# Attention of a decoder block: fewer and wider transfers, row maxima split on GpSimd before they are transposed, row scores in four one-head buffers

## What is computed

```python
q = (x @ Wqa @ Wqb).reshape(b, s, 16, 16)                 # 16 heads of 16 numbers
kv = (x @ Wkva @ Wkvb).reshape(b, s, 4, 16, 2)            # 4 heads of keys and values
q, k = _rope(q), _rope(kv[..., 0]); v = kv[..., 1]
k, v = jnp.repeat(k, 4, axis=2), jnp.repeat(v, 4, axis=2) # each serves a group of 4 query heads
scores = jnp.einsum('bqhd,bkhd->bhqk', q, k) * scale
scores = jnp.where(causal, -jnp.inf, scores)
out = jnp.einsum('bhqk,bkhd->bqhd', jax.nn.softmax(scores), v).reshape(b, s, 256) @ Wout + bout
```

## Time and profile before

| | us |
|---|---|
| median of 3 runs (lowest to highest) | 1511.91 (1509.64 to 1512.24) |
| the profiled execution, its own time | 1514.28 |
| its span in the profile | 1512.5 |
| PE busy with matmuls | 1118.5 (74%) |
| DVE busy | 787.8 (52%) |
| ACT busy | 659.5 (44%) |
| POOL busy | 341.5 (23%) |

### The profile page before, as it was taken

The page is one execution under the profiler, slowest core; times in us unless marked ns, Lnnn a source line. Parts: engine busy times, 40 slices in busy tenths (PEclk is TensorE's granted clock), DMA queues, the critical chain, the costliest instruction groups (busy, mean ns, idle before and its releaser), DMA issues. The chain is left out here.

```text
span 1512.5 us, 22735 instructions
## 1 busy us (share of the span) xinstructions
PE 1118.5 (74%) x7069; PEld 811.0 (54%) x7069; DVE 787.8 (52%) x1406; ACT 659.5 (44%) x1130; POOL 341.5 (23%) x466
## 2 busy tenths in 40 slices
PE   4773367777777786456543669999999999999875
PEld 2442123333333332356442558787777878787764
DVE  4886344555555551354424346565564646573623
ACT  1333034445545555213221344656556474746342
POOL 1432344553222222100101022112030404040300
PEclk9677578999999998657855879999999999999987
DMA  2333322221111100313433020303030202010000
GB/s 76 94 106 104 120 88 82 81 85 65 59 57 58 57 18 18 110 43 127 167 137 116 1 98 1 111 0 111 0 111 0 97 14 97 14 55 15 1 15 15
DMA packets 58876, 99.28 MB, mean 66 GB/s; under 512 B 8568, under 2 KB 43136, under 8 KB 54720
## 3 DMA queue, kind: packets, MB, share of 16 engines
q1 hardware_dynamic: 55852, 91.83, 18.1%
q0 software_dynamic: 1920, 6.03, 1.3%
q10 hardware_dynamic: 1044, 0.66, 0.2%
HBM read 62.45 MB, written 35.65 MB: 65 GB/s over the span
## 5 line engine op out<-in xcount | busy, mean ns | idle before, releaser
L777 ACT ACTIVATE p_probs<-p_psS 128x512 f32<-128x512 f32 (+1 forms) x352 | 187.6, 558 | 239.0 <-ACTq L776 239.0
L692 DVE TENSOR_REDUCE p_mx<-p_psA 128x2 f32<-128x1024 f32 (+3 forms) x256 | 202.3, 822 | 171.6 <-DVEq L691 171.6
L807 PE MATMUL p_psA<-p_ks,p_qs 96*128 96x384 bf16 (+3 forms) x512 | 142.7, 331 | 79.1 <-PEq L803 79.1
L1709 DVE TENSOR_TENSOR p_hl<-p_h,p_hh 128x512 fp32r<-128x512 f32 x128 | 87.0, 689 | 155.5 <-DVEq L1708 153.5
L827 PE MATMUL p_psS<-p_qs,p_ks 99*128 99x256 bf16 (+3 forms) x512 | 125.0, 318 | 41.4 <-PEq L852 41.4
L717 POOL TENSOR_SCALAR_AFFINE_SELECT p_probs<-p_probs 128x512 f32<-128x512 f32 x128 | 81.1, 634 | 240.0 <-POOLq L716 197.2
L1594 ACT ACTIVATE p_h<-p_psG,w_columns 128x512 f32<-128x512 f32 x128 | 88.3, 690 | 99.7 <-ACTq L1593 99.3
L807 PEld LDWEIGHTS p_psA<-p_ks,p_qs 96*128 96x128 bf16 x512 | 53.9, 105 | 127.5 <-issue 114.6
L809 PE MATMUL p_psA<-p_mask_b,p_ident_b 128*128 128x128 bf16 x512 | 111.8, 237 | 0.0
L1920 PE MATMUL p_psY<-p_n,p_hh 128*128 128x256 f32 x512 | 104.6, 288 | 3.0 <-PEq L1980 2.7
L827 PEld LDWEIGHTS p_psS<-p_qs,p_ks 99*128 99x128 bf16 x512 | 43.6, 100 | 112.7 <-issue 103.2
(11 more groups left out here) (246 smaller groups left out, 2766.5 us busy)
## 6 DMA issues: line engine op xcount, KB each, us to landing
p_n<-n_parts SPq DMA_DIRECT2D x16, 1024.0 KB, 6.7
n_parts<-p_nh SPq DMA_DIRECT2D x8, 1024.0 KB, 3.9
n_parts<-p_nl SPq DMA_DIRECT2D x8, 1024.0 KB, 6.0
q_parts<-p_part SPq DMA_DIRECT2D x96, 64.0 KB
p_qs<-q_parts SPq DMA_DIRECT2D x32, 192.0 KB
o_sums<-p_o SPq DMA_DIRECT2D x128, 34.0 KB
p_x<-in_x_dram SPq DMA_DIRECT2D x8, 512.0 KB, 4.0
p_qs<-q_parts SPq DMA_DIRECT2D x32, 128.0 KB
```

The lines of the kernel that those rows point to most:

```text
L692: nc.vector.tensor_reduce(mx[:, h:h + 2, i], psA[buffer_of(g, n)][:, :, 0:P * (i + 1)], AX_X, ALU.max).then_inc(A_free, 1)
L777: nc.scalar.activation(probs[:, g % 2, at:at + n * w], psS[(g * UNITS + s) % SB][:, 0:n * w], ACT.Exp, scale=SCALE).then_inc(exp_done, 1)
L807: nc.tensor.matmul(psA[buf][:, z, 0:n], qs[0:SROWS, k, h, i * P:(i + 1) * P], ks[0:SROWS, k, g, 0:n], start=True, stop=False)
L1709: nc.vector.tensor_tensor(hl[:, s, :], h[:, s, :], hh[:, s, :].bitcast(F32), ALU.subtract).then_inc(h_parts, 1)
```

## The change

Self-attention and the stores that feed it are written differently; nothing else is touched.

1. *Transfers.* SP issues 28 a batch in attention instead of 56. The queries are loaded as before, three transfers a group. Keys and values are loaded for two groups at once (L612, L615 of the changed kernel), four transfers for each half of a batch; those of the first two batches are issued by ACT. The maxima go with one transfer of 48 rows, `3x16x128` (L637). The result goes with one store of all 128 partitions (L643) into a scratch tensor of that shape. The scratch tensors of queries, keys and values are laid out anew, and projection stores a batch with 10 transfers, not 16.
2. *Maxima.* POOL splits `mx` into three parts as it stands, four operations on 128x16 (`split`), between the third and the fourth triangle of the group. PE transposes all three parts with one bfloat16 matmul (L833) into a bank of the ring `psS`, after row unit 0 of the next group; ACT copies them (`mrows`), SP moves them. They are turned one group ahead of their use, not two. DVE has no part in it any more.
3. *Row scores.* Four one-bank buffers `psA`, each with its own `A_free` and its own reduction: 16 reductions a group of one head each, not 8 of two.
4. *SP's order* in group g: maxima of g+1, store of g-1, refill. The queries of batch 1 are loaded in the groups of batch 0, not in front of it.

```diff
-                sp.dma_start(scr["v"][b].rearrange("g p n -> p g n"),
-                             v[:, k].rearrange("p g t n -> p g (t n)")).then_inc(v_out[k], 16)
+                sp.dma_start(scr["v"][b], v[:, k].rearrange("p g t n -> p (g t n)")).then_inc(v_out[k], 16)
...
-                            for z in range(2):
-                                g = 2 * u + z
-                                sp.dma_start(scr["q"][i, g, :, b, :].rearrange("d (h t) -> h d t", h=G),
-                                             part[i][z * G * D:(z + 1) * G * D, n, :]).then_inc(parts_out[n], 16)
+                            heads = slice(u * P // D, (u + 1) * P // D)
+                            sp.dma_start(scr["q"][i, :, b, heads, :].rearrange("d h t -> h d t"),
+                                         part[i][:, n, :]).then_inc(parts_out[n], 16)
...
-        psA = [ps(f"psA{i}", [P, 2, S]) for i in range(2)]
+        psA = [ps(f"psA{i}", [P, S]) for i in range(4)]
...
-                queue.dma_start(ks[rows, k, g, :], scr["k"][0:n, g * D:(g + 1) * D, b, :]).then_inc(stack_in[k][g], 16)
+                queue.dma_start(ks[rows, k, two].rearrange("p g t -> p (g t)"),
+                                scr["k"][0:n, b, :, two].rearrange("i d g t -> i d (g t)")).then_inc(kv_in[k][z], 16)
...
-                                 scr["q"][pq, g, :, b, :].unsqueeze(0).broadcast_to([n, D, G * S])).then_inc(stack_in[k][g], 16)
+                                 scr["q"][pq, :, b, heads, :].rearrange("d h t -> d (h t)").unsqueeze(0).broadcast_to([n, D, G * S])
+                                 ).then_inc(q_in[k][g], 16)
...
-                for i in range(MROWS):
-                    row = SROWS + i
-                    sp.dma_start(qs[row:row + 1, k, g * G:(g + 1) * G, :].rearrange("o h (t q) -> o (h t) q", t=TT),
-                                 mparts[i][:, g, :]).then_inc(m_in[g], 16)
+                sp.dma_start(qs[SROWS:SROWS + MROWS, k, g * G:(g + 1) * G, :].rearrange("i h t -> i (h t)"), mrows[:, g, :]
+                             ).then_inc(m_in[g], 16)
...
-                for r in range(G):
-                    sp.dma_start(scr["o"][b, g * G + r], o[32 * r:32 * r + D + 1, g % 2, :]).then_inc(o_out[g % 2], 16)
+                sp.dma_start(scr["o"][b, g], o[:, g % 2, :]).then_inc(o_out[g % 2], 16)
...
+            def split(g):
+                rows = mx[:, g * G:(g + 1) * G, :].rearrange("p h t -> p (h t)")
+                hi, mid, low = (msplit[:, g, i, :] for i in range(MROWS))
...
+            def maxima(bank, g):
+                pe.wait_ge(split_ready, 1)
+                pe.sem_inc(split_ready, -1)
+                nc.tensor.matmul(bank[0:MROWS * NG, 0:P], msplit[:, g].rearrange("p i x -> p (i x)"), ident_b[:, :],
+                                 start=True, stop=True).then_inc(S_ready, 1)
```

More of the change, by code:

```diff
@@ L597, in attend_phase, with place, load_keys @@
         ROWS_AT = [0, 1, 2, 3, 4, 6, 7, 8]
-        MAX_AT = 10
+        RING = len(SUNITS) + 1
+        TURN = 1
+        def place(s, turn=True):
+            return s + 1 if turn and s >= TURN else s
         block = ctx.enter_context(nc.Block())
-        def buffer_of(g, unit):
-            return (g * (len(AUNITS) + 1) + unit) % 2
-        def load_keys(queue, b, k, g):
+        def load_keys(queue, b, k, z):
+            two = slice(z * KVH // 2, (z + 1) * KVH // 2)
             row = 0
@@ L655, in batch @@
                         if has_next:
[L656 to L660 removed]
+                            refill(b + 1, 1 - k, KVH - 1)
+                    if first and g + 1 < KVH:
+                        load_queries(1, 1, g + 1)
             for g in range(KVH):
                 load_queries(0, 0, g)
[L664 to L667 removed]
+            maxima(0, 0)
+            load_queries(1, 1, 0)
             batch(0, 0, True, True, True)
@@ L782, in batch @@
                             out((g - 1) % KVH)
-            batch(True)
-            with act.Fori(1, B):
-                batch(False)
+            maxima(psS[0], 0)
+            batch(True, True)
+            with act.Fori(1, B - 1):
+                batch(False, True)
+            batch(False, False)
             out(KVH - 1)
@@ L860, in batch @@
-                    pe.sem_inc(m_in[g], -(16 * MROWS))
-                    for s in range(UNITS):
-                        n = start + s
-                        if n >= SB:
-                            exps(n - SB + 1)
-                        elif not first:
-                            exps(max(x for x in range(KVH * UNITS) if x % SB == n % SB) + 1 - KVH * UNITS)
-                        score_cols(k, g, s)
+                    pe.wait_ge(m_in[g], 16)
+                    pe.sem_inc(m_in[g], -16)
@@ L869, in batch @@
+                    for s in range(len(SUNITS)):
+                        if turn and s == TURN:
+                            maxima(ring(TURN, start), (g + 1) % KVH)
+                        score_cols(ring(place(s, turn), start), k, g, s)
                         if rows and s in ROWS_AT:
                             score_rows(*ahead, ROWS_AT.index(s))
-                        if rows and s == MAX_AT:
-                            maxima(ahead[1])
                         if s == PV2_AT and (g >= 1 or not first):
@@ L883, in batch @@
                             values(k, g, 1)
-                assert used[0] == WAITED
-            for g in range(AHEAD):
-                for unit in range(len(AUNITS)):
-                    score_rows(0, g, unit)
-                maxima(g)
+                return KVH * RING - (0 if has_next else 1) - used[0]
+            for unit in range(len(AUNITS)):
+                score_rows(0, 0, unit)
+            maxima(psS[0], 0)
+            pe.wait_ge(exp_done, 1)
+            pe.sem_inc(exp_done, -1)
@@ L890, in _ @@
+            for unit in range(len(AUNITS)):
+                score_rows(0, 1, unit)
             pe.wait_ge(minus_set, 1)
```

229 lines of the change are left out of this document (117 added, 112 removed).

## The result

The changed kernel takes **1454.1 us** in the median (1451.6 to 1457.7), the one before 1512.1 (1509.6 to 1515.7) beside it: ratio 0.9616, interval 0.9588 to 0.9645. The forecast was 1446, with a range from 1426 to 1478, and a chance of 0.96 for a faster kernel. The profiled execution took 1451.6 us with a span of 1449.8, the one before 1514.3 with 1512.5.

The account below looks back on a forecast made before the run. The first DMA engine, 306 KB or 12.0 us a group, was taken as the bound. Terms for groups, first batch, start and end summed to -65.7 us: 1514.3 to 1448.6 profiled, so 1446 us median, range 1426 to 1478.

Parts of the forecast that it names:

- The bound before: In steady groups the first DMA engine passes 306 KB at 26 GB/s, 12.0 us, setting the period of 12.2.
- The group after: Critical cycle between PE's matmuls of the maxima: 10.6 us a group, from 9.6 to 11.9.
- (b): PE's waits for row-score buffers ahead of units 4 and 6: 0.5 of 1.33 us left, bounds 0 and 1.33.
- (d): POOL's new split on 128x16, with hand-offs: 1.4 us a group, bounds 0.9 and 2.2.
- The new wait at L833: PE idle about 1.3 us a group ahead of the maxima's matmul, until POOL's split ends.
- the start: Start of attention: 5.5 us from fewer stores, 5 back for batch 1's keys, row scores 4; -4, bounds 0 and -9.
- The quicker row scores some 4: Before the first maxima: quicker first row scores bring the start some 4 us forward.
- Later phases: Phases after attention: no changed transfer on their path, so 0 us.
- A: POOL's split is shorter or hidden: groups of 9.6 to 10.0 us, kernel 1422 or 1434 us; chance 0.17.
- B: First DMA engine still sets the pace: maxima land late, refilled groups 11.7 us, kernel 1471 us; chance 0.14.
- C: Slower than before: maxima landing in 11 us make groups of 14.4 us, kernel 1551 us; chance 0.03.
- D: Something unseen holds groups at 12.2 us; only start, first batch and end change, 1490 to 1510 us; chance 0.04.

Follow-up runs that it names:

- run 1: The kernel before with the wide store alone, one transfer of 128 rows a group instead of four of 17: 1467.1 us, ratio 0.9694.
- run 2: The changed kernel with the four stores of 17 rows put back and the scratch tensor in its old shape: 1511.9 us, ratio 0.9993.
- run 7: The changed kernel with query transfers cut to 16 rows each without the broadcast, six a group instead of three: 1439.8 us, ratio 0.9515.
- run 3: The changed kernel with the first copy of POOL's split made three times, a longer split: 1483.5 us, ratio 0.9804.
- run 4: The changed kernel with POOL's split moved ahead of the third triangle: 1432.5 us, ratio 0.9462.
- run 6: The changed kernel with PE's matmul of the maxima one step later: 1440.4 us, ratio 0.9516.
- run 8: The changed kernel with the second batch's keys and values issued by SP behind the first maxima, not by ACT at the start: 1445.5 us, ratio 0.9562.
- run 5: The changed kernel with row scores in two buffers of two heads again, each freed by one reduction: 1481.2 us, ratio 0.9781.
- run 12: The kernel before with the wide store and four row-score buffers of one head, keeping the old split and two groups of lead: 1434.2 us, ratio 0.9456.
- run 11: The kernel of run 9 with the split's four operations on DVE behind its last reduction, not on POOL: 1429.4 us, ratio 0.9446.
- run 9: The changed kernel with the split ahead of the third triangle and query and key transfers cut to 16 rows: 1403.2 us, ratio 0.9287.

## Why the prediction was right, and where it was off

- **The bound before**: right. Runs 1 and 2 move 120 KB a group off or on one engine, and groups go between 12.2 and 10.8, between 10.4 and 12.3. The sum for run 2, 309 KB at 26 GB/s or 12.1 us, comes within 2%. The trace doesn't name the engine of a packet: that one engine is full follows from packet counts, sizes and these runs. The number of transfers, changed with it, is excluded by run 7.
- **The group after**: forecast 10.6, measured 10.43. (b) the buffers' waits: 0.5 left forecast, 0.31 measured. (d) the split: 1.4 forecast, 1.36 measured. The new wait at L833: 1.3 forecast, 1.05 measured. Run 3 shows that it is serial, run 4 that most of it goes once the split is moved, run 6 that it goes when the turn is later and mostly comes back at the values. That half of what the buffers give is paid back was low: 0.73 of 1.09. The upper bound of the group's sum, 11.9, doesn't follow from its terms: with no wait gone and the split at 2.2 they add up to 12.2. DVE's busy time was forecast to rise to 7.7 us a group and stayed at 6.8 (81.18/12; 6.9 before), so this sign of being right did not appear; nothing hung on it, since DVE doesn't set the group.
- **The sums**, measured against forecast: steady twelve -21.3 (-19.2), eight with weights -19.8 (-18), six further -6.7 (-5.5), last two +1.8 (+2), first batch -14.6 (-16), end -6.1 (-5, from the last exponential to the next phase).
- **The step that failed is the start**: -4 forecast, +1.4 measured, outside its bounds of 0 and -9. With the later phases it makes 8.2 us, of which the better groups gave back 5; the profiled execution missed by 3.0 (1451.6 against 1448.6), so that the close total is in part luck: two errors offset each other. Two of its three terms came out: SP free 5.6 earlier (5.5), and the keys of the second batch 5.0, by run 8 (5). The first came out by luck, since twelve transfers fewer at 0.58 us would be 7.0 and not 5.5. "The quicker row scores some 4" is the term that failed. PE did finish sooner: it is through with what stands ahead of the first step at 186.2, 33.3 us after attention begins, where the first step came after 35.9 us before. But it then waited 7.94 us for the landing, so that nothing of this counts: the first step comes 41.3 us after the beginning, and 40.2 to 41.2 in runs 2 to 6, which have the same loads. The forecast added up gains and losses of two paths, PE's and the transfers', of which only the longer one sets the start. What stood ahead of the landing were keys (run 8) and queries of four groups, as run 7 shows by spreading them, -9.5. Not in the forecast at all was a longer gap before attention begins, 4.0 us and not 2.4. Its cause stays open, but it goes with the changed projection: the kernels with the old stores there have 2.4 to 2.6 (before, runs 1 and 12), all others 3.8 to 4.4.
- **Later phases**: 0 forecast, +2.8 measured. Kernels whose code is the same from there on scatter as much: from the last exponential to the end of the span 909.6 us in run 8, 919.2 in run 7, 914.2 in the changed kernel, with a mean granted clock of 0.73, 0.71 and 0.71 in the first 369 us of it. I ascribe nothing to the change there. The beginning of attention scatters as well, from 149.5 to 153.8 us in the eleven kernels with the changed projection, so that a start is better counted from there.
- **Rivals.** A's time of 1434 came true, but by moving the split (run 4), not in the change itself. B was wrong for the steady stretch (run 7: 12 groups in 125.6 with 81 KB) and right for the start and the first batch, where its mechanism cost 14 us; I had priced it at the wrong place. C and D fell: groups are 10.4 with maxima landed in time.

The Trainium skill's rule that a leading broadcast of c copies confines a transfer to at most c engines ("DMA: Bandwidth & Descriptors", "Use all 16 engines") speaks against a form that the change keeps. Run 7 agrees, with 14.3 us; what decides is that these transfers stand ahead of something waited for, since in the steady groups the same cut gives nothing.

## What to carry to other kernels

Add up the bytes of each transfer by the engines that it is really shared by, and look at the fullest one; a mean DMA share of 0.18 hid a full engine. Of a change in several parts, run each alone: here one gave 45 us, one 27, and one cost 0.7 us a group, some 20 in all. Before you move an operation to another queue, ask what stands before and behind it there: the same split is worth 22 us more ahead of a triangle than behind it. And add up a start by paths: a gain on the shorter one brings nothing.

## What the runs showed of the hardware

- *DVE waits for POOL.* Operations of 0.17 us on DVE took 0.58 and 0.66 beside a POOL triangle and ended with it (run 11), while the reductions of 512 numbers, which read PSUM, kept their 0.69. The Trainium skill states a lock for this ("SBUF — State Buffer", "SBUF: two separate sides"): a port pair shared by DVE and GpSimd is held for a whole instruction, against DVE operations with two SBUF inputs or in a two-port mode. For the subtraction, with two SBUF inputs, the trace agrees. The cast has one, and whether it ran in such a mode the trace doesn't say.
- *A wait can cost more than itself.* At a wait of 1.87 us a group, 0.82 us more of PE idle time a group brought the granted clock from 1.00 to 0.92 and as much again in PE's busy time (run 3), while the changed kernel, with 1.13 us idle at that place, kept 1.00. Where the clock stayed at 1.00, a wait counted once: 0.67 us more of it made the group 0.62 longer (run 11 against 9), 0.76 less made it 0.72 shorter (run 4).
- *Three kernels meet at 9.7.* Runs 4, 9 and 12, with different splits and different transfers, all take 9.70 to 9.73 us a group, PE busy 9.0 to 9.1 of it at a clock of 1.00. In all three PE is idle for 3.7 us in 12 groups at the row scores, and for 3.5, 4.0 and 5.2 us at the maxima's matmul or transposition. What would remove these 0.6 to 0.7 us a group was not tried.
